# One fused transformer block: the end of a top-k routing step rearranged around the last batches of a shared network

## The chip, the cores and the metric

The kernel runs on one core of a Trainium2 chip. The metric is the device time of one execution in microseconds (us). The five engines of the core run their own instruction streams and wait for each other by semaphores: TensorE (PE, matmuls), VectorE (DVE), ScalarE (ACT), GpSimd (POOL) and SyncE (SP, which here only issues DMA transfers).

## The reference

The block takes 8 batches of 512 tokens with 256 features. Two conditioned layer norms stand ahead of a 16-head latent attention and of a mixture of experts; both results are added to the stream, scaled by gates. Only the second half matters here:

```python
scores = sigmoid(h @ gate_w.T)                 # 4096 tokens, 16 experts
topk_score, topk_ids = top_k(scores.T, 512)    # each expert takes its 512 best tokens
xin = h[topk_ids]
eo = silu(xin @ gw + gb) * (xin @ up_w + up_b) # F = 1024
eo = (eo @ down_w + down_b) * topk_score
out = zeros.at[topk_ids].add(eo)
shared = (silu(h @ sh_gate) * (h @ sh_up)) @ sh_down   # 512 wide, every token
x = x + gb_gate * (out + shared)
```

## The kernel before

The program has three parts in time: attention over 16 units of 8 heads (to about 440 us), the shared network over 8 batches (to about 610 us), and the 16 experts (to the end). Matmuls are made of three passes over values split into a high and a low part; ScalarE writes the high part, VectorE or POOL the low part. For a weight this split is called `cut`: ScalarE copies a quarter of a loaded piece, VectorE subtracts. An expert's gate, up and down weights are pieces of 1 MB that pass through two raw buffers, `WR`.

The shared network is a list of 48 steps, `ORDER`, and all five engines walk through it, `w` being the step's number. A step is either `glu(b, i)`, a quarter of the gate and up products of batch b (12 matmuls of 512 columns), or `down(b, i)`, half of its down product (24 matmuls of 256 columns). For b of 1 and more the order is glu 0, glu 1, glu 2, down(b-1, 0), glu 3, down(b-1, 1). So batch 6 begins at step 34 and batch 7 at step 40, and steps 46 and 47 are the down steps of batch 7. After a glu step, VectorE multiplies the two products into `HF` (L1688), ScalarE makes its high part `HTh`, POOL its low part `HTl` (L1925). After each quarter of a down step, VectorE makes the output rows: `tb` from the product and the gate row `GBt` (L1698), then `EO` as the sum with the batch's x2, `XL` (L1703). When a batch is done, SP stores `EO` and loads the next batch's `GBt` and `XL` into the same buffers (`store_out`, `load_xl`). `load_h` loads the split hidden state of a later batch into `XT`. Between steps 18 and 32 SP also copies gate rows into the table of token rows (`load_gate_rows`), 512 KB each.

From step 10 on the top-k runs between these products. Each engine counts ticks, four in a step; every third tick is a step `t` of the top-k. TensorE's ticks stand behind every third matmul of a glu step's quarter and behind each half of a down quarter. First the threshold of each expert is found bit by bit: VectorE counts the scores above a candidate (L1578), TensorE sums over partitions (L810), VectorE sets or drops the bit (L1567, L1570). At T_SEL VectorE marks scores above and equal to the threshold, at T_TIE it admits as many equal ones as are needed and runs a second prefix sum (`tensor_tensor_scan`, L1603), for which TensorE makes the offsets over partitions (L817). At T_POS the positions are formed and transposed by TensorE (L821). At T_VAL, T_HOT and T_VAL1, T_VAL2 VectorE makes, first for expert 0 and then for the others, the row and column of each position (`rows`), one-hot rows `OH` (`onehot`, four parts for an expert, L1661) and the token numbers as values `V4` (`values`). `index(x)` is 32 small matmuls of `OH` and `V4` (L877), from which VectorE writes `IDX` (L1671); POOL then gathers the 512 token rows of the expert into `XG` with four indirect DMAs (L1932). `turn(x, ck)` transposes them on TensorE (L892) and splits them into `XT`.

Each engine executes in order. The end of the list on VectorE reads:

```python
if w == W_INDEX:
    index(0)
...
if W_PIECES <= w < W_PIECES + 8:     # steps 39 to 46: gate and up weights of expert 0
    cut(e, piece_g(0) + j // 4, j % 4)
if w in (42, 43, 44, 45):
    onehot(1, w - 42)
```

The memory of expert 0's up weights holds the tables of the top-k until these are used up; the memory of its gate weights is free once the last batch's attention output is stored.

## Time and profile before

| | |
|---|---|
| median of 3 runs | 1196.64 us (1192.25 to 1196.66) |
| the profiled execution | 1189.41 us, its span 1187.7 us |
| busy share of the span | PE 94%, DVE 73%, POOL 53%, ACT 50% |
| mean granted TensorE clock | 0.966 of full speed |

The span goes from the first to the last instruction. Rows of a timeline show start and duration in us, engine, source line, operation, what is written and read, shape and count; brackets at the end give the time for which the engine stood idle before the row, and what it waited for. PE's durations overlap each other by a part of each matmul.

### The profile page before, as it was taken

Reading aid. Unit: us, or ns where it says so; the run is one execution under the profiler, and the core shown is the slowest. Engines: PE = TensorE matmul, PEld = TensorE weight load, DVE = VectorE, ACT = ScalarE, POOL = GpSimd, SP = SyncE. Lnnn points to the kernel's source line nnn. Section 1 sums busy time; section 2 is a strip of 40 time slices with the busy share of each in tenths; the row PEclk is TensorE's granted clock in tenths of the full one; section 3 lists DMA queues with packets and bytes.
Section 4 is the critical chain, followed back from the end, with each engine's and each line's share of the span. In section 5 each row is a group of like instructions: output and inputs, shape, how many; then the busy total and the mean of one; then the engine's idle time right before and its main releaser. Section 6 shows DMA issues by size and latency. Waiting matters only on the chain.

```text
span 1187.7 us, 21663 instructions
## 1 busy us (share of the span) xinstructions
PE 1115.0 (94%) x7463; PEld 868.7 (73%) x7464; DVE 865.0 (73%) x2213; ACT 596.9 (50%) x1083; POOL 634.0 (53%) x669
## 2 busy tenths in 40 slices
PE   7789989998988998998989999999999999999997
PEld 5455645555555567887778888888888888888886
DVE  5587888796877868887967767667767667767562
ACT  2257767776676654222334454344454444454441
POOL 4134476574665734222426656666656656656644
PEclk8788999998999999999989999999999999999999
DMA  7646677868668644857345555554455655455531
GB/s 192 89 72 118 109 122 161 175 126 173 132 149 167 175 149 130 256 183 212 95 141 122 139 155 132 145 135 127 135 154 133 143 136 126 136 154 134 139 81 18
DMA packets 100333, 165.44 MB, mean 139 GB/s; under 512 B 18424, under 2 KB 65016, under 8 KB 98176
## 3 DMA queue, kind: packets, MB, share of 16 engines
q1 hardware_dynamic: 83360, 137.04, 45.5%
q0 software_dynamic: 14336, 25.70, 11.2%
q10 hardware_dynamic: 2528, 1.32, 0.9%
q8 instruction: 60, 0.98, 0.4%
q14 instruction: 49, 0.40, 0.1%
HBM read 103.71 MB, written 34.11 MB: 116 GB/s over the span
## 4 chain that ended last, share of the span: by engine, by line
PE 58%; DVE 12%; DMA 10%; POOL 6%; issue 6%; SPq 3%; ACT 3%; ACTq 1%; DVEq 0%; POOLq 0%
PE MB L551 15%; PE LB L551 14%; PE LB L865 8%; PE MB L865 8%; DMA HT<-Us 3%; DVE junk L1319 3%; SPq L332 2%; PE XB L551 2%; PE LB L643 2%; PE UB L681 2%; PE UB L551 2%; POOL out_y L1967 2%; DMA rdD<-D 2%; DMA XT<-hD 1%; DMA DN<-rdD 1%
## 5 line engine op out<-in xcount | busy, mean ns | idle before, releaser
L1925 POOL TENSOR_TENSOR HTl<-HF,HTh 128x512 fp32r<-128x512 f32 x156 | 217.5, 1400 | 211.0 <-ACT HTh L1078 210.6
L1319 DVE CUSTOM_DVE_ANT_0 junk<-MB,MK 128x256 bf16<-128x256 f32 (+3 forms) x512 | 219.7, 483 | 62.7 <-PE MB L620 61.5
L1831 POOL TENSOR_SCALAR_AFFINE_SELECT P<-P 128x256 f32<-128x256 f32 x256 | 101.8, 422 | 153.8 <-ACT P L1017 153.6
L1967 POOL DMA_INDIRECT out_y<-EO,IDX x64 | 108.8, 1699 | 76.1 <-DVE EO L1787 66.0
L1089 ACT ACTIVATE SIL<-LB,gbT 128x512 f32<-128x512 f32 x64 | 43.9, 685 | 193.7 <-PE LB L551 193.7
L1015 ACT ACTIVATE P<-LB 128x768 f32<-128x768 f32 x128 | 103.7, 811 | 72.7 <-PE LB L643 72.5
L620 PE MATMUL MB<-KS,QS 48*128 48x256 f32 (+3 forms) x512 | 129.4, 365 | 9.9 <-DMA KS<-ST 4.7
L643 PE MATMUL LB<-QS,KS 50*128 50x256 f32 (+3 forms) x512 | 123.2, 358 | 15.4 <-ACT P L1015 12.5
L1078 ACT ACTIVATE HTh<-HF 128x512 fp32r<-128x512 f32 x156 | 97.8, 627 | 66.7 <-DVE HF L1688 66.4
L643 PEld LDWEIGHTS LB<-QS,KS 50*128 50x128 f32 x512 | 79.3, 192 | 63.4 <-issue 51.2
L620 PEld LDWEIGHTS MB<-KS,QS 48*128 48x128 f32 x512 | 81.4, 196 | 22.1 <-DVE NM L1319 12.4
L865 PE MATMUL LB<-WDh,HTh 128*128 128x256 f32 x320 | 94.0, 294 | 3.8 <-DVE tb L1698 3.8
L1688 DVE SCALAR_TENSOR_TENSOR HF<-MB,ubT,SIL 128x512 f32<-128x512 f32 x64 | 47.7, 745 | 66.0 <-ACT SIL L1089 30.4
L1661 DVE TENSOR_TENSOR OH<-R,iotab 128x1024 bf16<-128x1024 bf16 x64 | 93.1, 1458 | 0.0
L865 PE MATMUL MB<-WDh,HTh 128*128 128x256 f32 x320 | 92.0, 288 | 0.5 <-DVE tb L1698 0.5
L681 PE MATMUL UB<-P,V 128*32 128x512 f32 (+3 forms) x1024 | 90.9, 476 | 0.9 <-POOL P L1831 0.6
L865 PE MATMUL MB<-WDl,HTh 128*128 128x256 f32 x320 | 91.2, 285 | 0.0
L865 PE MATMUL MB<-WDh,HTl 128*128 128x256 f32 x320 | 91.1, 285 | 0.0
L865 PE MATMUL LB<-WDh,HTl 128*128 128x256 f32 x320 | 91.0, 284 | 0.0
L865 PE MATMUL LB<-WDl,HTh 128*128 128x256 f32 x320 | 91.0, 284 | 0.0
L1932 POOL DMA_INDIRECT XG<-tab,IDX x64 | 64.9, 1013 | 39.9 <-DVE IDX L1671 25.4
L1688 DVE SCALAR_TENSOR_TENSOR HF<-LB,ubT,SIL 128x512 f32<-128x512 f32 x64 | 47.7, 745 | 50.1 <-PE LB L551 50.1
(312 smaller groups left out, 3040.8 us busy)
## 6 DMA issues: line engine op xcount, KB each, us to landing
WR<-in_gw SPq DMA_DIRECT2D x16, 1024.0 KB, 7.6
WR<-in_uw SPq DMA_DIRECT2D x16, 1024.0 KB, 4.9
WR<-in_dw SPq DMA_DIRECT2D x16, 1024.0 KB, 5.5
QS<-ST SPq DMA_DIRECT2D x96, 128.0 KB, 4.6
KS<-ST SPq DMA_DIRECT2D x90, 128.0 KB, 5.9
hD<-h SPq DMA_DIRECT2D x8, 1024.0 KB, 5.8
XT<-hD SPq DMA_DIRECT2D x7, 1024.0 KB, 9.0
X<-in_x SPq DMA_DIRECT2D x8, 512.0 KB, 6.3
```

Source lines behind the costliest of these rows:

```text
L551: m = e.matmul(ps, a(c), r(c), start=(i == 0), stop=(i == 5))
L620: m = e.matmul(MB[:, o:o + w], QS[base:base + 48, k, i * 128:(i + 1) * 128], KS[base:base + 48, k, 0:w], start=True, stop=True)
L643: m = e.matmul(LB[:, o:o + w], KS[base:base + 50, k, j * 128:(j + 1) * 128], QS[base:base + 50, k, 128 * j:512], start=True, stop=True)
L681: m = e.matmul(UB[32 * h:32 * h + 32, 128 * j:512], V[b % 2][:, j, 8 * c + 4 * g + h, :], P[(8 * u + 4 * g + h) % NP][:, o:o + w], start=( ...
L865: m = e.matmul(ps, a[:, slots[f], ts], r[:, f, :], start=(f == 0 and t_ == 0), stop=(f == len(slots) - 1 and t_ == 2), skip_group_check=True)
L1015: e.activation(P[n % NP][:, 512:1280], LB[:, 512:1280], ACT.Exp).then_inc(a_p, 1)
L1078: e.activation(HTh[:, slot, :], hf_of(n)[:], ACT.Copy).then_inc(a_ht, 1)
L1319: m = e.tensor_tensor_reduce(junk[:, o:o + w], MB[:, o:o + w], MK[:, 512 - w:512], 1.0, -3e38, ALU.add, ALU.max, NM[:, k // 4, 4 * (k % 4) ...
L1688: e.scalar_tensor_tensor(out=hf_of(n)[:], in0=up, scalar=bias, in1=sil_of(n)[:], op0=ALU.add, op1=ALU.mult).then_inc(d_hf, 1)
L1831: m = e.affine_select(out=dd, in_=dd, compare_op=ALU.is_ge, fill=0.0, base=0, pattern=[[0, 2], [1, 128]], channel_multiplier=-1)
L1925: e.tensor_tensor(HTl[:, slot, :], hf_of(n)[:], HTh[:, slot, :].bitcast(F32), ALU.subtract).then_inc(g_ht, 1)
L1967: e.indirect_dma_start(out=out2, out_offset=bass.IndirectOffsetOnAxis(ap=IDX[x_ % 3][:, q:q + 1], axis=0), in_=EO[:, q, :], in_offset=None ...
```

## The change

The tie step's second matmul and all steps after it move by one top-k step: T_TIE keeps its work on VectorE, but TensorE takes its result one step (three ticks) later, and T_POS, T_VAL and the others follow one step later than before. The values of experts 1 to 15 are made in two halves in two steps. The first index moves from step 40 to 41 on all engines, and POOL's two halves of the first gather with it. The four cuts of expert 0's gate weights move to steps 18, 20, 22 and 24, those of its up weights are at steps 42 to 45. The down weights of expert 0 are loaded at step 34 instead of 43. Two of the four one-hot parts of expert 1 move into the first two quarters of expert 0; the second index moves there from quarter 1 to 2, and the one-hots of expert 2 by one quarter. The hidden state of batches 4 to 7 is loaded one step earlier. The last batch's x2 and gate row have buffers of their own, `XL7` and `GB7`, and are loaded at step 16.

```diff
 T_SEL = T_BIT + 31
-T_TIE, T_POS, T_VAL, T_HOT, T_VAL1, T_VAL2, T_END = (T_SEL + i for i in (1, 2, 3, 4, 6, 8, 9))
+T_TIE, T_POS, T_VAL, T_HOT, T_VAL1, T_VAL2, T_END = (T_SEL + i for i in (1, 3, 4, 5, 7, 8, 10))
+N_TIE, N_POS, N_VAL, N_ALL = (T_SEL + i for i in (2, 3, 4, 7))
...
 W_LOAD = 13
-W_PIECES = 39
-W_INDEX = 40
+W_CUTS = (18, 20, 22, 24, 42, 43, 44, 45)
+W_INDEX = 41
...
     SC6 = at("SC6", 50048, [128, 512])
+    XL7 = at("XL7", 33664, [128, 4, D])
+    GB7 = at("GB7", 37760, [128, D])
     VR = at("VR", 69504, [128, 8])
...
     c_gbt, c_xl, c_out, c_sco, c_pos, c_scat = (sem(n) for n in ("c_gbt", "c_xl", "c_out", "c_sco", "c_pos", "c_scat"))
-    c_sd = sem("c_sd")
+    c_sd, c_l7 = sem("c_sd"), sem("c_l7")
...
             e.dma_start(outv[b], EO[:]).then_inc(c_out, 16)
-            if b + 1 < NB:
+            if b + 2 < NB:
                 load_xl(b + 1)
...
                 store_split(NB - 1)
-            if kind == "glu" and i == 1 and 3 <= b < NB - 1:
+            if kind == "glu" and i == 0 and 3 <= b < NB - 1:
                 load_h(b + 1)
+            if w == 16:
+                e.wait_ge(c_xd, 16 * NB)
+                e.wait_ge(g_sd, 2)
+                e.dma_start(GB7[:], modD[NB - 1, 5:6, :].broadcast_to([128, D])).then_inc(c_l7, 16)
+                e.dma_start(XL7[:], xD[NB - 1]).then_inc(c_l7, 16)
             if w == 15:
...
                 e.dma_start(WR[1][:].rearrange("p (k n) -> p k n", k=2), kn(uw[0])).then_inc(c_wr[1], 16)
-            if w == W_PIECES + 4:
+            if w == 34:
                 load_piece(piece_d(0), dw[0])
...
                 e.matmul(XB[:, 2:3], Lm, PT[:, 511:512], start=True, stop=True).then_inc(p_top, 1)
-            elif t == T_TIE:
-                e.wait_ge(d_top, t + 1)
+            elif t == T_TIE + 1:
+                e.wait_ge(d_top, N_TIE)
                 e.matmul(XB[:, 3:4], Lm, PT[:, 511:512], start=True, stop=True).then_inc(p_top, 1)
             elif t == T_POS:
-                e.wait_ge(d_top, t + 1)
+                e.wait_ge(d_top, N_POS)
                 for k in range(4):
...
-            e.wait_ge(d_top, T_VAL + 3 if x_ else T_VAL + 1)
+            e.wait_ge(d_top, N_ALL if x_ else N_VAL)
             for k in range(32):
...
                 glu(n_eglu(x_, m_) - 1, m_, WG[x_ % 2], WU[x_ % 2], XT[x_ % 2], no_tick)
-                if nxt and m_ == 1:
+                if nxt and m_ == (1 if x_ else 2):
                     index(x_ + 1)
...
                 flush()
-            if W_PIECES <= w < W_PIECES + 8:
-                j = w - W_PIECES
+            if w in W_CUTS:
+                j = W_CUTS.index(w)
                 cut(piece_g(0) + j // 4, j % 4)
...
                 if t == T_HOT:
-                    e.wait_ge(d_top, T_VAL + 1)
+                    e.wait_ge(d_top, N_VAL)
                 onehot(0, 2 * (t - T_HOT))
                 rows(slice(1, NE), d_top)
-            elif t == T_VAL2:
-                values(slice(1, NE))
+            elif t in (T_VAL2, T_VAL2 + 1):
+                values(slice(1, NE), range(2 * (t - T_VAL2), 2 * (t - T_VAL2) + 2))
...
-        def values(es):
-            for q in range(4):
+        def values(es, qs=range(4)):
+            for q in qs:
                 e.tensor_scalar(of(V4[:, q, 0, :], es), of(GT[:], es), float(q), VR[:, 0:1], ALU.is_equal, ALU.mult)
...
             e.wait_ge(p_down, n)
-            e.wait_ge(c_gbt, 16 * (b + 1))
-            e.tensor_tensor(tb[q % 2][:], (LB, MB)[q % 2][:, 1024:1280], GBt[:], ALU.mult).then_inc(d_tb, 1)
+            last = b == NB - 1
+            if last:
+                e.wait_ge(c_l7, 32)
+            else:
+                e.wait_ge(c_gbt, 16 * (b + 1))
+            e.tensor_tensor(tb[q % 2][:], (LB, MB)[q % 2][:, 1024:1280], (GB7 if last else GBt)[:], ALU.mult).then_inc(d_tb, 1)
             e.wait_ge(d_tb, n)
-            e.wait_ge(c_xl, 16 * (b + 1))
+            if not last:
+                e.wait_ge(c_xl, 16 * (b + 1))
             if b:
                 e.wait_ge(c_out, 16 * b)
-            e.tensor_tensor(EO[:, q, :], tb[q % 2][:], XL[:, q, :], ALU.add).then_inc(d_eo, 1)
+            e.tensor_tensor(EO[:, q, :], tb[q % 2][:], (XL7 if last else XL)[:, q, :], ALU.add).then_inc(d_eo, 1)
...
                     shared_down(b, q)
-            if W_PIECES <= w < W_PIECES + 8:
-                j = w - W_PIECES
+            if w in W_CUTS:
+                j = W_CUTS.index(w)
+                if j == 4:
+                    e.wait_ge(d_top, N_ALL)
                 cut(e, piece_g(0) + j // 4, j % 4)
-            if w in (42, 43, 44, 45):
-                onehot(1, w - 42)
+            if w in (43, 45):
+                onehot(1, (w - 43) // 2)
         for x_ in range(NE):
                 glu(n_eglu(x_, m_) - 1, m_, ubT[:, x_, m_:m_ + 1])
+                if x_ == 0 and m_ < 2:
+                    onehot(1, 2 + m_)
                 if m_ < 4:
                     cut(e, piece_d(x_), m_)
-                if nxt and m_ == 1:
+                if nxt and m_ == (1 if x_ else 2):
                     index(x_ + 1)
                     cut(e, piece_g(x_ + 1), m_ - 4)
-                if x_ + 2 < NE and 2 <= m_ < 5:
-                    onehot(x_ + 2, m_ - 2)
+                if x_ + 2 < NE and (2 if x_ else 3) <= m_ < (5 if x_ else 6):
+                    onehot(x_ + 2, m_ - (2 if x_ else 3))
                 if nxt and m_ >= 6:
...
                     glu(n_eglu(x_, m_ - 1) - 1, m_ - 1, m_ - 1, n_edown(x_, 0) - 1)
-                if m_ == 1 and x_ + 1 < NE:
+                if m_ == (1 if x_ else 2) and x_ + 1 < NE:
                     index(x_ + 1)
             if x_:
```

## Rows read from the trace of the kernel before

**Rows 1.** Windows: busy us by engine, with instructions; then clock, DMA share, GB/s.

```profile
500.00:551.00 51.00, 50.88 (x313) 44.96 (x312) 40.88 (x121) 12.41 (x22) 14.19 (x11) 1.00 0.67 199
...
561.00:565.00 4.00, 4.00 (x12) 3.11 (x13) 1.51 (x3) 1.08 (x2) 0.00 (x0) 0.57 0.07 29
...
599.70:605.00 5.30, 5.23 (x24) 5.23 (x25) 4.16 (x7) 0.13 (x1) 0.81 (x1) 0.50 0.39 111
```

**Rows 2.** Timeline of PE, 552 to 612 us, the rows that begin with idle time.

```profile
552.37 0.72 PE L551 MATMUL LB<-XT,WG1h 128*128 128x512 f32 x2 [1.49 <-DMA XT<-hD]
...
560.96 0.38 PE L817 MATMUL XB<-PT,C 128*128 128x1 f32 x2 [2.36 <-DVE PT L1603]
...
575.84 0.99 PE L877 MATMUL UB<-V,OH 128*128 128x8 bf16 x32 [1.03 <-DVE OH L1661]
...
585.70 0.73 PE L551 MATMUL LB<-XT,WU1h 128*128 128x512 f32 x2 [1.91 <-DVE HF L1688]
...
594.90 0.39 PE L865 MATMUL MB<-WDh,HTh 128*128 128x256 f32 x1 [0.51 <-DVE tb L1698]
...
599.77 0.58 PE L865 MATMUL LB<-WDh,HTh 128*128 128x256 f32 x1 [2.60 <-DVE tb L1698]
...
607.21 0.39 PE L865 MATMUL LB<-WDh,HTh 128*128 128x256 f32 x1 [1.16 <-DVE tb L1698]
```

**Rows 3.** Timeline of DVE at the ties.

```profile
556.45 0.16 DVE L1594 TENSOR_SCALAR sm<-XB 128x1 f32<-128x1 f32 x1 [0.34 <-PE XB L814]
...
558.74 2.17 DVE L1603 TENSOR_TENSOR_SCAN PT<-GT,SC 128x512 f32<-128x512 f32 x1
```

**Rows 4.** DMA issues, KB and us to landing: issues of 534 to 541, then 497 to 501.

```profile
XT<-hD SPq DMA_DIRECT2D x1, 1024.0 KB, 15.8
```

```profile
XT<-hD SPq DMA_DIRECT2D x1, 1024.0 KB, 8.2
```

**Rows 5.** Chain of work that ended last, 470 to 700 us: start, us, what.

```profile
592.97 1.44 PE LB L865 x12
...
613.47 2.80 PE MB L551 x12
```

**Rows 6.** Timeline of DVE, 565 to 595 us.

```profile
565.57 0.69 DVE L1611 TENSOR_SCALAR PT<-UB 128x512 f32<-128x512 f32 x1 [2.64 <-PE UB L821]
...
568.92 2.36 DVE L1661 TENSOR_TENSOR OH<-R,iotab 128x1024 bf16<-128x1024 bf16 x2
...
575.71 0.40 DVE L1636 TENSOR_SCALAR GT<-PT 128x480 f32<-128x480 f32 x1
...
578.70 0.41 DVE L1698 TENSOR_TENSOR tb<-LB,GBt 128x256 f32<-128x256 f32 x1
...
580.29 0.68 DVE L1797 TENSOR_TENSOR WG0l<-WR,WG0h 128x512 fp32r<-128x512 f32 x1
...
581.08 0.16 DVE L1671 SCALAR_TENSOR_TENSOR IDX<-sm 128x4 uint32<-128x4 f32 x1
...
584.39 0.65 DVE L1646 SCALAR_TENSOR_TENSOR V<-GT,VB 128x480 bf16<-128x480 f32 x1
...
591.21 3.31 DVE L1703 TENSOR_TENSOR EO<-tb,XL 128x256 f32<-128x256 f32 x1
```

**Rows 7.** Timeline of POOL, 582 to 592 us.

```profile
582.19 1.46 POOL L1932 DMA_INDIRECT XG<-tab,IDX  x1 [8.96 <-DVE IDX L1671]
...
584.95 3.00 POOL L1925 TENSOR_TENSOR HTl<-HF,HTh 128x512 fp32r<-128x512 f32 x2
...
589.66 2.00 POOL L1932 DMA_INDIRECT XG<-tab,IDX  x1 [0.30 <-issue]
```

**Rows 8.** Tile XG, 575 to 640 us: us from issue to landing of its transfers.

```profile
DMA to landing us min/median/max: 3.6/3.8/6.8
```

**Rows 9.** Timelines of DVE and of PE at one bit step.

```profile
514.03 0.75 DVE L1578 TENSOR_SCALAR_CACHE_REDUCE jk<-S,si 128x512 bf16<-128x512 f32 x1
```

```profile
514.94 0.28 PE L810 MATMUL XB<-sm,C 128*128 128x1 f32 x2
```

## The prediction

> **What bounds the kernel now.** The windows come first. From 500 to 551 us TensorE has no gap to speak of: 50.88 of 51.00 us busy at clock 1.00 [rows 1]. So the bit steps of the top-k, shown as matmuls of one column between those of the shared network, cost it next to nothing, and what is added there costs only if a bit step comes late. Then TensorE's own timeline, read for the idle time in brackets: from 551 to 610 there are seven waits of over 0.5 us, one for a DMA and six for VectorE, 1.49 + 2.36 + 1.03 + 1.91 + 0.51 + 2.60 + 1.16 = 11.1 us [rows 2]. Back to the windows: two of the waits, 2.36 and 2.60, are followed by a stretch near or at the lower clock level, 4.00 us at 0.57 and 5.30 us at 0.50 [rows 1], where work that takes the full clock 2.3 and 2.65 us takes 4.00 and 5.30: 1.7 + 2.65 = 4.35 us lost. After waits of 1.49, 1.03 and 1.91 us no such stretch follows. So 15.4 us stand open between 551 and 610 us. Everything the diff touches either lies there or is moved out of there. VectorE's timeline [rows 3, 6] shows why it waits: VectorE does the ties, the rows, the one-hots and the values of the top-k one after another between the products that TensorE needs.
>
> **The hidden state of batch 6 (load_h one step earlier).** The transfer that TensorE waits for at 552.37 took 15.8 us to land; it stood behind a 512 KB copy of gate rows. The one for batch 4, issued just after the same output store and x2 load but ahead of all gate rows, took 8.2 [rows 4]. Moved to step i == 0 it is issued ahead of the gate rows of its own step. With a landing between 8 and 13 us (estimated from these two rows, with one copy less ahead) it is there by 549 and the wait goes. Bounds: 0 and 1.49 us gained. I take 1.4, less what the bit steps below lose, because a TensorE that arrives later waits less.
>
> **The ties in two steps.** TensorE's 2.36 us wait is for the second scan. VectorE's tie work runs from 556.45 to 560.91 (558.74 + 2.17) [rows 3]: 4.5 us, started by a TensorE matmul three products into step 35. Before, TensorE had nine products to do until it needed the scan; with the change it has eighteen. Twelve take 2.80 us [rows 5], so nine take 2.1: the second nine cover 2.1 of the 2.36, and about 0.4 is left with the small matmuls between. A wait of 0.4 is shorter than any that the clock fell after. Gain 1.9 plus the 1.7 of the slow stretch: 3.6 (bounds 1.9, if the clock falls all the same, and 4.1).
>
> **Everything behind the ties, three ticks later.** The position transposes move from step 36 to the middle of step 37; all of the top-k after them follows. I count from the end of these transposes. VectorE then does: value step of the first expert 2.75 (565.57 to 568.92, less a product of 0.60), a pair of shared outputs 1.6 (578.70 to 580.29), four one-hot quarters 4.6 (two in 2.36), a product 0.6, half a pair 0.8, the rows of the other experts 2.4 (575.71 to 578.70, less a product), half a pair 0.8, half the values 1.9 (eight from 581.24 to 585.04, halved), a product 0.6 [rows 6]. Together 16.1 us to the product of step 40, and 0.35 more to the index at the start of step 41. On top come collisions with POOL's split: a sum of two SBUF tiles beginning at 591.21 took 3.31 us where such a sum takes 0.4, while POOL ran without a break [rows 6, 7]. I add 1.0 (0 to 2.5).
>
> The Trainium skill says under "SBUF — State Buffer", section "Who interferes with whom", that a VectorE instruction with two SBUF inputs and a GpSimd one that reads SBUF exclude each other for a whole instruction. By that rule one-hots and weight splits, which have two SBUF inputs, could each lose up to a POOL split of 1.3 to 1.5 us, and the sum would tend to its upper end; the 3.31 us row agrees.
>
> TensorE meanwhile does 1.4 (half of step 37), 2.8, 2.9, 2.8 (steps 38 to 40), the first index 0.9, 2.8 (41), and half of step 42, 1.4: 15.0 us (12 gate/up products 2.80, 12 down products 1.44 [rows 5]; the index's 32 matmuls are the 0.99 us row at 575.84 [rows 2], 0.9 as the next ones overlap its end). There it needs the product of step 40, at 17.1: a wait of about 2 where 1.91 stood before (0.5 to 3.5). The wait of 1.03 for the one-hots goes: they are done 10.7 after the transposes, the index matmuls start at about 9.9 to 10; I keep 0.5 for it.
>
> **The first expert's gather.** VectorE's index stands at about 17.5. POOL then needs 0.95 to begin, two gathers 2.75 (582.19 to 584.95), two splits of the shared network 3.0, then 1.7 (587.95 to 589.66) to the issue of the last, and its landing: 3.8 us in the middle, 6.8 at worst [rows 7, 8]. The last gather lands 12 to 15 after the index, 29.5 to 32.5 after the transposes. TensorE comes to the turn of the gathered rows at 15.0 + 2.5 of waits + 1.4 + 2.9 + 2.8 + 2.9 = 27.5. So a wait of 2 to 5 us appears at step 46, which before had none. I take 2.5: the 1 MB down-weight load that ran beside the last gathers is now at step 34, and 3.8 is the nearer price. After a wait of that length the clock fell both times before; I take half of the second stretch's loss, 1.3 (0 to 2.65).
>
> **Gate weights among the bits.** A split is one ScalarE copy and one VectorE subtraction of 0.68 [rows 6]; four leave the crowded steps and go to steps 18, 20, 22 and 24. On VectorE the split of step 20 falls ahead of the count at 514.03, which ends at 514.78, and TensorE uses it at 514.94 [rows 9]: 0.16 of slack against 0.6 of work, so 0.5 us lost. At the other three the slack is larger. I take 0.5 (0 to 2.7, four whole splits). Removing them from the end is already in the sum above: steps 39 to 42 hold no gate splits.
>
> **x2 of the last batch in its own place.** Its two loads leave the end of step 45 for step 16, two more issues on SP, behind load_h and ahead of gate rows that are due only at the gather. The 1.16 us wait at 607.21 hangs on the late loads and goes; behind it only the output store of batch 6 is late, and I keep 0.3. The waits of 0.51 and 2.60 us are for VectorE's order and its 3.31 us sum; what is left of them is in the gather's wait above.
>
> **First expert.** Half the one-hots and the index of the second expert move there, one step later. VectorE was not the bound there; the gather is issued some 2 us later and is still down before its turn, four quarters of 2.8 us further on. I cost this at nothing; without that cover it is up to 2 us.
>
> **Sum.** Open before 15.4; left after: ties 0.4, one-hots 0.5, the product of step 40 2.0, gather 2.5, clock 1.3, end 0.3, bits and load_h 0.6, in all 7.6. So about 8 us come off. The span of 1187.7 becomes 1179.7; the profiled execution's 1189.41 becomes 1181.4. The median of the runs is 7.2 us above the profiled execution, so the forecast for it is 1196.6 − 8 = 1188.6, its own range 1185 to 1192.
>
> **Rivals.** *The gather decides all* (0.20): the index late by more collisions or a landing of 6.8, the clock down the whole 2.65. Wait 5 in place of 2.5, clock 2.65 in place of 1.3, other terms as above: gain 4, 1192.6, no difference to be told. For it: POOL's row of work without a break [rows 7]. Against: no weight load beside it now. *More than summed* (0.13): the gather in time and no fall of the clock: gain 8 + 2.5 + 1.3, about 12, 1184.6 or less. For it: TensorE's pure work behind the ties is fixed. *Slower* (0.05): the clock. Four waits of 0.4 to 2.5 us in 30 us of work; if it stayed at the lower level from step 42 to the first expert, about 17 us of full-clock work would take 17 more, 1205.6 in all. From 8 us of such work on nothing is gained, from 14 on the kernel is slower. Against: both stretches of before ended after 4 to 5.3 us, the last waits notwithstanding [rows 1]. *Change without effect*: not a case by itself; the 1.49 and 2.36 us waits have their cause in the order that is edited.
>
> The forecast has 0.62. What a measurement can tell is about 0.5%, 6 us, and the forecast stands only 2 us inside that. Faster by more: 0.62 + 0.13 less 0.04 at the forecast's edge, 0.71; within 0.5%: 0.24; slower 0.05. The range, 1180 to 1194, runs from below the better case to beyond the first rival.
>
> **To be seen in the profile after.** No wait for the hidden state before step 34; under 1 us at the tie matmul and no slow stretch behind it; a wait of 1 to 3 us at step 42's up half for the product of step 40; one of 2 to 5 us at the first turn, for the gathered rows; no wait for the last batch's x2. Wrong would make it: several bit steps late at 500 to 551 us, the gather landing later than 33 us after the position transposes, or experts longer than before.

## The result and the profile after

The changed kernel takes 1183.80 us (median of 12 runs, 1181.54 to 1194.76) against 1192.67 (12 runs, 1188.40 to 1201.29) for the kernel before beside it: ratio 0.9929, 95% interval 0.9901 to 0.9957. The medians are 8.9 us apart; the interval does not reach 1. The profiled executions, by which the prediction counted, went from 1189.41 to 1181.54 us, their spans from 1187.7 to 1179.8: 7.9 us less, where 8 were foreseen.

For everything below one stretch is used, called the stage: from the first bit sum that TensorE waits for behind 490 us to the first gate matmul of expert 0. It took 118.83 us before (491.59 to 610.42) and 111.34 after (491.33 to 602.67), so 7.5 of the 7.9 us came off there. The experts are the same: from the stage's end to the end of the span 577.28 us before and 577.13 after, the first expert 35.81 and 35.70.

The timeline of TensorE in the changed kernel, 510 to 604 us, the rows that begin with idle time (they answer to [rows 2]):

```profile
515.19 0.38 PE L821 MATMUL XB<-sm,C 128*128 128x1 f32 x2 [0.34 <-DVE jk L1590]
...
559.89 0.27 PE L829 MATMUL XB<-PT,C 128*128 128x1 f32 x1 [0.37 <-DVE PT L1615]
...
573.09 0.99 PE L889 MATMUL UB<-V,OH 128*128 128x8 bf16 x32 [0.36 <-DVE OH L1673]
...
581.15 0.74 PE L562 MATMUL LB<-XT,WU1h 128*128 128x512 f32 x2 [2.82 <-DVE HF L1700]
...
592.92 0.66 PE L904 MATMUL XB<-C,XG 128*128 128x128 f32 x4 [1.25 <-DMA XG<-tab,IDX]
...
594.86 0.39 PE L877 MATMUL LB<-WDh,HTh 128*128 128x256 f32 x1 [1.29 <-DVE tb L1714]
...
599.71 0.38 PE L877 MATMUL LB<-WDh,HTh 128*128 128x256 f32 x1 [1.00 <-DVE tb L1714]
```

These are seven waits, 7.43 us together, and no stretch at the lower clock; the prediction left 7.6 us of waits and lost clock. The one for the hidden state is gone, the tie's is 0.37 for 2.36, the one-hots' 0.36 for 1.03. The product of step 40 costs 2.82 instead of 1.91. The gather has a wait that it did not have before, and two waits for `tb` stand at the end, both behind late VectorE work.

The transfers of the hidden state, issued at 534 to 545 us, KB and us to landing (they answer to [rows 4]):

```profile
XT<-hD SPq DMA_DIRECT2D x1, 1024.0 KB, 9.9
```

VectorE's timeline of the changed kernel, rows at the bit step of step 20 and between 567 and 600 us (they answer to [rows 6] and [rows 9]):

```profile
512.61 0.68 DVE L1820 TENSOR_TENSOR WG0l<-WR,WG0h 128x512 fp32r<-128x512 f32 x1
...
514.38 0.75 DVE L1590 TENSOR_SCALAR_CACHE_REDUCE jk<-S,si 128x512 bf16<-128x512 f32 x1
...
567.32 5.72 DVE L1673 TENSOR_TENSOR OH<-R,iotab 128x1024 bf16<-128x1024 bf16 x4
...
574.78 2.33 DVE L1651 SCALAR_TENSOR_TENSOR GT<-PT,GT 128x480 f32<-128x480 f32 x2
...
581.20 0.16 DVE L1683 SCALAR_TENSOR_TENSOR IDX<-sm 128x4 uint32<-128x4 f32 x1
...
586.47 0.69 DVE L1700 SCALAR_TENSOR_TENSOR HF<-LB,SIL 128x512 f32<-128x512 f32 x1 [2.61 <-POOL HTl L1948]
...
589.69 2.45 DVE L1820 TENSOR_TENSOR WU0l<-WR,WU0h 128x512 fp32r<-128x512 f32 x1
...
594.84 1.34 DVE L1720 TENSOR_TENSOR EO<-tb,XL 128x256 f32<-128x256 f32 x1
...
599.89 0.43 DVE L1720 TENSOR_TENSOR EO<-tb,XL 128x256 f32<-128x256 f32 x1 [0.24 <-DMA out_y<-EO]
```

One row of the kernel before, with which the row of 2.33 us is compared:

```profile
576.14 1.35 DVE L1639 SCALAR_TENSOR_TENSOR GT<-PT,GT 128x480 f32<-128x480 f32 x2
```

POOL's timeline of the same kernel, 566 to 592 us (it answers to [rows 7]):

```profile
566.99 1.56 POOL L1948 TENSOR_TENSOR HTl<-HF,HTh 128x512 fp32r<-128x512 f32 x1 [4.54 <-ACT HTh L1090]
574.38 1.52 POOL L1948 TENSOR_TENSOR HTl<-HF,HTh 128x512 fp32r<-128x512 f32 x1 [5.83 <-ACT HTh L1090]
582.30 1.44 POOL L1955 DMA_INDIRECT XG<-tab,IDX  x1 [6.40 <-DVE IDX L1683]
584.05 0.97 POOL L1955 DMA_INDIRECT XG<-tab,IDX  x1 [0.31 <-issue]
585.04 2.56 POOL L1948 TENSOR_TENSOR HTl<-HF,HTh 128x512 fp32r<-128x512 f32 x2
...
589.31 0.95 POOL L1955 DMA_INDIRECT XG<-tab,IDX  x1 [0.30 <-issue]
590.28 1.30 POOL L1948 TENSOR_TENSOR HTl<-HF,HTh 128x512 fp32r<-128x512 f32 x1
```

Lay VectorE's and POOL's rows side by side. The four one-hots begin 0.33 us after a POOL split began and take 5.72 where [rows 6] give 4.6; the pair of rows at 574.78 begins 0.40 after the next split and takes 2.33 where the same two took 1.35 (576.14 in the kernel before); the 2.45 us weight split, 0.68 elsewhere, holds all of the POOL split of 590.28. And at 586.47 VectorE stands 2.61 us because POOL makes the low part of batch 7's first quarter only after the first two gathers.

### The profile page after: what moved, and what is told of

Same layout as the page of the kernel before. It is cut to its first block, busy times and chain, and to the rows that moved or that the text cites. A ratio compares the mean times of both kernels' runs of the same rounds, so it can differ in the third digit from the quotient of the medians.

```text
span 1179.8 us, 21665 instructions
## 1 busy us (share of the span) xinstructions
PE 1111.8 (94%) x7464; PEld 867.0 (73%) x7464; DVE 866.5 (73%) x2213; ACT 597.2 (51%) x1083; POOL 633.0 (54%) x669
## 4 chain that ended last, share of the span: by engine, by line
PE 62%; DVE 12%; DMA 6%; issue 6%; POOL 6%; ACT 4%; SPq 2%; ACTq 1%; DVEq 0%; POOLq 0%
PE MB L562 16%; PE LB L562 15%; PE LB L877 8%; PE MB L877 8%; DVE junk L1331 3%; PE UB L562 3%; PE LB L654 3%; PE XB L562 2%; DMA HT<-Us 2%; PE UB L692 2%; POOL out_y L1990 2%; SPq L337 1%; ACTq L1019 1%; POOL hl L1846 1%; DMA rdD<-D 1%
## 5 line engine op out<-in xcount | busy, mean ns | idle before, releaser
L692 PE MATMUL UB<-P,V 128*32 128x512 f32 (+3 forms) x1024 | 87.4, 461 | 0.7 <-POOL P L1854 0.4
```

Source lines behind the costliest of these rows:

```text
L692: m = e.matmul(UB[32 * h:32 * h + 32, 128 * j:512], V[b % 2][:, j, 8 * c + 4 * g + h, :], P[(8 * u + 4 * g + h) % NP][:, o:o + w], start=( ...
```

## The experiments

Each kernel is the changed one with an edit; each has one profiled execution, called its trace here. The whole time of a single execution varies by more than what is sought (1181.54 to 1194.76 us in the twelve of the change), so the traces are read by their stage. The change itself was run a second time (`after_again`): its stage is 110.47, so differences of under 0.9 us say nothing by themselves.

```
             stage  VectorE  clock, 4 us  what is altered
                    busy     behind the wait at step 42
before       118.83  98.65
after        111.34  97.24   1.00
after_again  110.47  96.62   0.57
u_load       111.43  96.77   0.62         hidden state one step later again
u_tie        114.64  97.40   1.00         ties in one step again
u_cuts       112.61  96.95   0.59         gate splits at steps 39 to 46 again
u_x2         115.17  96.91   0.60         x2 of the last batch as before
u_hot        112.31  98.45   0.61         four one-hots of expert 1 at 42 to 45
p_pool       111.15  98.94   1.00         first split ahead of the gathers
p_late       111.38  99.18   1.00         last value tables one step later
p_both       111.21  99.02   1.00         both, four gathers in a row
n_hot        107.97  93.23   0.58         no one-hot of expert 1 in the stage
n_hot2       108.54  93.36   0.58         the same, index of expert 1 later
n_hot2_late  108.04  94.89   1.00         n_hot2 with p_late
```

Clock is the granted clock of the windows view, a mean over the 4 us. At step 42 TensorE waits 2.82 to 2.85 us in nine of these traces; in six of them the clock then fell to 0.57 to 0.62 for 4 us, in three it stayed at 1.00. At 0.57 such a fall loses about 1.7 us where it stands, and later waits give part of it back (the wait for the gather was there in `after`, not in `after_again`). So each kernel is compared with the trace of the change that has the same clock there: 111.34 at 1.00, 110.47 at the lower one. This pairing was made after the traces were seen, and rests on one trace of the change at each clock.

The column shows step 42 alone. Four kernels have a further slow stretch before expert 0, which neither trace of the change has: `u_cuts` 0.62, `u_x2` 0.57 and `u_hot` 0.62, each for 4 us, and `p_both` 0.50 for 5.2 us. By these clocks it is worth some 1.5, 1.7, 1.5 and 2.6 us, an estimate, and it is part of what their stages show.

**u_load.** The hidden state is loaded at the step where it was before.

```diff
-            if kind == "glu" and i == 0 and 3 <= b < NB - 1:
+            if kind == "glu" and i == 1 and 3 <= b < NB - 1:
```

> The changed kernel with the hidden states of batches 4 to 7 loaded at i == 1 again; all else as changed. The stage is read from the matmul of the first bit sum that shows a wait (about 491 us) to the first matmul of expert 0: 118.8 us before, 111.3 changed. Theory (the transfer stood behind gate rows and set step 34): TensorE waits 1.3 to 1.6 us for the hidden state at step 34 again, and the stage is 1.0 to 1.5 us longer, 112.3 to 112.8. Rival (VectorE's count and mark work at the threshold is late anyway and hides it): no more than 0.4 longer.

Measured:

```profile
558.71 0.73 PE L562 MATMUL LB<-XT,WG1h 128*128 128x512 f32 x2 [0.98 <-DMA XT<-hD]
```

The wait is back with 0.98 us, and TensorE reaches step 42's product 0.95 later, counted from the stage's start (90.77 for 89.82), so nothing in between takes it up. It is less than the 1.49 of before because TensorE comes to it 0.6 later in the stage (59.89 for 59.29), while the transfer lands at the same place (60.87 and 60.78). The stage is 0.96 longer than that of `after_again`; against the 111.3 from which the expectation counts it is only 0.1 longer, as the rival has it.

**u_tie.** Both tie steps in one.

```diff
-            elif t == T_TIE + 1:
+            elif t == T_TIE:
```

> The changed kernel with TensorE's second tie matmul in the tie step itself, as before; the later top-k steps stay one step later. Theory: TensorE waits 2.4 to 2.7 us there in place of 0.37, everything behind is late by it: stage 2.0 to 2.3 us longer, 113.3 to 113.6; if the clock falls again after that wait, up to 1.7 more, 115.3. Rival (VectorE's row of work up to step 42 sets the end, so that TensorE's earlier wait is only moved): the 2.82 us wait at step 42 shrinks by what the tie wait grows, stage within 0.5 of 111.3.

Measured, two views of this kernel: TensorE's timeline, and the window behind its first row.

```profile
563.47 0.58 PE L829 MATMUL XB<-PT,C 128*128 128x1 f32 x2 [2.36 <-DVE PT L1615]
```

```profile
563.50:567.50 4.00, 4.00 (x12) 3.29 (x13) 1.40 (x3) 0.65 (x2) 0.00 (x0) 0.59 0.98 362
```

The wait of 2.36 is back to the hundredth, and so is the slow stretch of 4 us; at 0.59 it loses 1.6. The stage is 3.30 longer than the change's at the same clock later on. The prediction had 3.6, and this expectation up to 115.3 with the clock's fall.

**u_cuts.** The gate splits go back into steps 39 to 46, and the down-weight load with them.

```diff
-W_CUTS = (18, 20, 22, 24, 42, 43, 44, 45)
+W_CUTS = (39, 40, 41, 42, 43, 44, 45, 46)
...
-            if w == 34:
+            if w == 43:
```

> The changed kernel with the eight weight splits of expert 0 at steps 39 to 46 and its down weights loaded at step 43 again. Theory (VectorE is the bound from the transposes to the first index): two splits of 0.6 to 1.25 us stand ahead of the first index; the wait for the product of step 40 grows by 0.6 to 1.25, the index is 1.2 to 2.5 later, the last gather lands that much later, and the 0.34 us wait among the bits goes: stage 0.9 to 2.2 longer, 112.2 to 113.5. Rival (TensorE waits behind for POOL, not for VectorE's sum of work): stage 0.3 shorter.

Measured:

```profile
593.45 0.73 PE L562 MATMUL LB<-XT,WU1h 128*128 128x512 f32 x2 [3.43 <-DVE HF L1700]
...
608.21 1.11 PE L904 MATMUL XB<-C,XG 128*128 128x128 f32 x4 [3.10 <-DMA XG<-tab,IDX]
```

There is no wait at the bit steps of steps 18 to 24; the wait at step 42 is 3.43 and that for the gathered rows 3.10, with the clock at 0.59 and 0.62 behind them. The stage is 2.1 longer than `after_again`, a second slow stretch included. The splits and the down-weight load were put back together, so their shares are not told apart.

**u_x2.** The last batch's x2 is loaded into the buffers of the batch before, as it was.

```diff
-            if b + 2 < NB:
+            if b + 1 < NB:
                 load_xl(b + 1)
...
-            if w == 16:
+            if w == -1:
...
-            last = b == NB - 1
+            last = False
```

> The changed kernel with the last batch's x2 and gate row loaded into the shared buffers after the output store of batch 6, as before. Theory of the prediction: about 1.2 us, the wait of before at the second half of the last down step, less the 1.0 that stands there now: stage up to 1.2 longer, 111.3 to 112.5. Rival (now that the end is earlier, the load is on the path: store at 597.0, landing of the gate row 4.5 us after its issue at about 597.5, so the product with it at 602 in place of 599.2): 2.5 to 3.5 longer, 113.8 to 114.8.

Measured, VectorE's and then TensorE's timeline at step 46 of this kernel:

```profile
601.13 0.42 DVE L1714 TENSOR_TENSOR tb<-LB,GBt 128x256 f32<-128x256 f32 x1 [3.04 <-DMA GBt<-modD]
602.35 0.43 DVE L1720 TENSOR_TENSOR EO<-tb,XL 128x256 f32<-128x256 f32 x1 [0.80 <-DMA XL<-xD]
```

```profile
601.61 0.39 PE L877 MATMUL LB<-WDh,HTh 128*128 128x256 f32 x1 [4.14 <-DVE tb L1714]
```

SP issues the two loads at 596.27 and 596.76 and VectorE can go on at 601.13 and 602.35. The wait of 1.16 in [rows 2] was the visible end of this; with the other waits taken out ahead of it, TensorE comes there earlier, the wait is 4.14 and the clock falls to 0.57 for 4 us behind it. The stage is 4.7 us longer than that of `after_again` (3.8 longer than that of `after`), above the rival's 113.8 to 114.8 too, and far more than the 0.86 that the prediction read off the 1.16.

These four and `u_hot` (below), each undone alone, cost 0.96 + 3.30 + 2.1 + 4.7 + 1.8 = 12.9 us, against 7.5 to 8.4 that the whole change brings. The parts do not add up. The second slow stretches of `u_cuts`, `u_x2` and `u_hot`, about 4.7 us by the estimate above, are about as large as the surplus; whether one wait also hid part of the next in the kernel before is not shown. The later first index and the halved values were not undone alone.

**p_pool, p_late, p_both.** These try to remove what is left. In `p_pool` POOL makes the low part of batch 7's first quarter ahead of the first two gathers; in `p_late` the last value tables go from step 40 to the step after, behind the product of step 40; `p_both` does both and issues all four gathers in a row. Cuts from the edits:

```diff
 # p_late
-... for i in (1, 3, 4, 5, 7, 8, 10))
+... for i in (1, 3, 4, 5, 7, 9, 11))
 # p_pool: index(0, (0, 1)) moved behind the glu that precedes it on POOL
```

> The changed kernel with one order on POOL turned round: at step 41 the low part of batch 7's first quarter first, then the first two gathers of expert 0. Theory (VectorE's product of step 42 stands 2.61 us for that low part, which is queued behind the two gathers, and the waits of 1.29 and 1.00 us at the last down steps follow from it): VectorE's 2.61 us falls under 0.6, the two waits of TensorE together from 2.3 to under 0.6, the last gather lands about 0.8 later, and expert 0 begins 1.5 to 2.5 earlier: stage 109 to 110 where the clock stays up. Rival (the gather is what the end hangs on): expert 0 begins 0 to 0.8 later, stage 111.3 to 112.1. If the clock falls after the wait at step 42, as in three of the five looks so far, up to 1.6 more by either.

> The changed kernel with the values of experts 1 to 15 made one top-k step later, behind the product of step 40 and the first index on VectorE. Theory (VectorE's row of work from the transposes to that product is what TensorE waits for at step 42, and the index behind it sets the gather): the wait at step 42 goes from 2.82 to 0.8 to 1.0, the index is 1.9 us earlier, the last gather lands as much earlier, stage 1.5 to 2.0 shorter, 109.3 to 109.8. Rival (the low part on POOL behind the gathers sets the end, whatever is earlier on VectorE): stage within 0.5 of 111.3.

> Both at once, and all four gathers of expert 0 together behind the low part at step 41. Theory: the wait at step 42 under 1.0, POOL: low part to about 88.7 us from the stage's start, four gathers to 94, the last landing at 98 to 98.9; TensorE comes to the turn at 98.5 to 99, so no wait there over 0.5; no waits over 0.6 at the last down steps; stage 105.5 to 107, that is 4 to 6 us under the changed kernel, ratio to the kernel before 0.988 to 0.990. Rival (the gathers' issue or landing slows when four follow each other, or VectorE is late for the turn): stage 108 to 110, ratio 0.991 to 0.993.

Measured: the wait of VectorE (`p_pool`) or of TensorE at step 42 (`p_late`, `p_both`) that was aimed at went each time, and the stage, 111.15, 111.38 and 111.21, did not move. Rows of VectorE in `p_pool`:

```profile
585.48 1.50 DVE L1657 TENSOR_SCALAR V<-GT,VR 128x480 bf16<-128x480 f32 x1
...
589.47 1.77 DVE L1820 TENSOR_TENSOR WU0l<-WR,WU0h 128x512 fp32r<-128x512 f32 x1 [0.69 <-ACT WU0h L1075]
...
592.77 2.44 DVE L1820 TENSOR_TENSOR WU0l<-WR,WU0h 128x512 fp32r<-128x512 f32 x1
```

The 2.61 us idle row is gone, but 0.69 is now spent waiting for ScalarE's half of a split, a value row takes 1.50 for 0.46, and two weight splits take 4.21, where the change itself spent 3.52 on them (1.07 + 2.45) and two undisturbed ones take 1.36. TensorE's waits behind step 42 are 1.16 for the gathered rows and 1.35 and 0.99 for `tb`, as in the change. In `p_late` the wait at step 42 was 0.93 as expected, and waits of 0.53, 1.25, 1.12, 1.40 and 0.98 followed. In `p_both`, VectorE, then POOL, then TensorE and the window behind its row:

```profile
594.30 3.61 DVE L1820 TENSOR_TENSOR WU0l<-WR,WU0h 128x512 fp32r<-128x512 f32 x1 [0.69 <-ACT WU0h L1075]
```

```profile
592.62 0.96 POOL L1955 DMA_INDIRECT XG<-tab,IDX  x1 [0.30 <-issue]
593.88 0.95 POOL L1955 DMA_INDIRECT XG<-tab,IDX  x1 [0.30 <-issue]
594.86 2.50 POOL L1948 TENSOR_TENSOR HTl<-HF,HTh 128x512 fp32r<-128x512 f32 x2
```

```profile
598.30 0.58 PE L877 MATMUL LB<-WDh,HTh 128*128 128x256 f32 x1 [3.59 <-DVE tb L1714]
```

```profile
598.30:602.30 4.00, 4.00 (x18) 4.00 (x19) 3.97 (x7) 0.43 (x1) 0.00 (x0) 0.50 0.00 0
```

One split of 0.68 us stands through both POOL splits, TensorE waits 3.59 for `tb`, and the clock is 0.50 behind it. Without that slow stretch (2.6 us by the estimate above) the stage would be about 108.6, in the rival's 108 to 110, so this trace alone does not show that nothing was won. `p_both` was also timed: 1186.76 (6 runs), ratio to before 0.9910 (0.9875 to 0.9945), not to be told from the change's. The theory that one wait sets the end fell here. The next one was that VectorE's whole work between the ties and the last down step sets it: in these three its busy time in the stage is 98.9 to 99.2 us, 1.7 to 1.9 above `after`; what VectorE no longer stood idle went into stretched rows.

**after_again.**

> The changed kernel unaltered, beside the others on the same chip: ratio to the kernel before 0.990 to 0.996. Stage 111 to 112 by the theory that its waits are fixed by order; the wait at step 42 between 2.75 and 2.9 either way, and the clock after it either at 1.00 or near 0.6.

Measured: 1186.17 us (10 runs), ratio to before 0.9918 (0.9892 to 0.9944); stage 110.47, half a us under the expected band, with 0.57 behind the 2.82 us at step 42, no wait for the gathered rows, and two for `tb`:

```profile
599.30 0.39 PE L877 MATMUL LB<-WDh,HTh 128*128 128x256 f32 x1 [0.69 <-DVE tb L1714]
...
604.14 0.39 PE L877 MATMUL LB<-WDh,HTh 128*128 128x256 f32 x1 [0.99 <-DVE tb L1714]
```

**u_hot, n_hot.** Two one-hots of the second expert are put back into the stage, or the two that are left are taken out. `u_hot` also puts the second expert's index and the third one's one-hots back by a gate step; those lie behind the stage.

```diff
 # u_hot
-            if w in (43, 45):
-                onehot(1, (w - 43) // 2)
+            if w in (42, 43, 44, 45):
+                onehot(1, w - 42)
...
 # n_hot
-            if w in (43, 45):
-                onehot(1, (w - 43) // 2)
...
-                    onehot(1, 2 + m_)
+                    onehot(1, 2 * m_)
+                    onehot(1, 2 * m_ + 1)
```

> All four one-hot rows of the second expert stand at steps 42 to 45 again, as in the kernel before; nothing else is altered. Two more rows of 1.16 us each enter VectorE's work between the first expert's one-hots and the last down step (2.3 us, up to 3.5 with waits behind GpSimd), and the same two leave the first expert's gate steps. Theory (the sum of VectorE's work in this stretch, not one wait of it, sets when the first expert begins): the stage, 111.3 in the profiled run after and 110.5 in its repeat, becomes 112.8 to 114.8, with the loss in front of the two last down products (tb), not at step 42. Rival (the gathers and GpSimd's queue set the end, VectorE has room): the stage stays within 110.4 to 111.8. The whole time of one look varies by 3 us and decides nothing here.

> All four one-hot rows of the second expert stand in the first expert's first two gate steps (two in each); none is left at steps 43 and 45. Two rows of 1.16 us leave VectorE's work before the first expert. Theory (the sum of VectorE's work sets the start of the first expert): the stage becomes 108.0 to 109.5 from 110.5 to 111.4, and the first expert, in which TensorE had no wait, is longer by 0 to 1 us; ratio of the whole to the kernel before about 0.991 (0.9929 measured for the change). Rival (the last gather, 11.7 us behind the index, takes over as the limit): the waits of the two tb shrink and one for the gathered rows grows; the stage stays at 110 to 111.4. Second rival: the second expert's index comes late by the two rows, its gather lands after its first turn, and up to 2.5 us return as a wait at the second expert's first gate step.

Measured: `u_hot` is 1.8 longer than `after_again`, outside the rival's band and half a us short of the theory's, with the loss in front of `tb` as the theory has it:

```profile
599.42 0.58 PE L877 MATMUL LB<-WDh,HTh 128*128 128x256 f32 x1 [2.66 <-DVE tb L1714]
```

The waits for `tb` grew by 1.0 (2.66 for 0.69 + 0.99); the rest of the 1.8 goes with the slow stretch of 0.62 behind this wait. `n_hot` is 2.5 shorter, at the lower end that the theory names, and without a wait behind step 42. The windows of the stage in the change and in `n_hot` (us, then busy us of PE, PEld, DVE, ACT and POOL, then clock):

```profile
491.33:602.67 111.34, 103.78 (x654) 90.45 (x655) 97.24 (x230) 28.90 (x51) 33.42 (x26) 1.00 0.61 180
```

```profile
498.05:606.02 107.97, 104.04 (x655) 91.71 (x655) 93.23 (x228) 29.01 (x51) 33.17 (x26) 0.98 0.61 185
```

VectorE is busy 3.4 to 4.0 us less than in the change's two traces, 2.4 of it the two rows, the rest stretched rows. In the stage the two kernels differ from the change in these rows of VectorE alone, and it moves by them both ways: that VectorE's work behind step 42 holds up the end of the stage is shown by this pair. That the sum of its busy time sets the stage is not: `p_pool`, `p_late` and `p_both` have 98.9 to 99.2 us and stages of 111.2 to 111.4, `u_hot` 98.45 and 112.31, `u_x2` 96.91 and 115.17. And the whole did not gain: TensorE's timeline of `n_hot` in the first expert:

```profile
617.78 0.99 PE L889 MATMUL UB<-V,OH 128*128 128x8 bf16 x32 [3.23 <-DVE OH L1673]
```

The first expert took 40.62 us for 35.70, 3.23 of it this wait for the one-hots and the rest at a clock of 0.55 to 0.59 for some 4 us behind it. Neither the 0 to 1 us of the theory nor the second rival's place (the turn) was right. 1185.70 us, ratio 0.9910 (0.9877 to 0.9943).

**n_hot2, n_hot2_late.** The one-hots are spread over three gate steps and the index follows one step later.

```diff
-                if nxt and m_ == (1 if x_ else 2):
+                if nxt and m_ == (1 if x_ else 3):
                     index(x_ + 1)
...
-                if x_ == 0 and m_ < 2:
-                    onehot(1, 2 + m_)
+                if x_ == 0 and m_ == 0:
+                    onehot(1, 0)
+                if x_ == 0 and m_ < 3:
+                    onehot(1, 1 + m_)
```

> As n_hot, with the second expert's one-hot rows at the first expert's gate steps 0 (two), 1 and 2 and its index one gate step later (after step 3), on every engine that takes part. Theory: the stage stays at 107.5 to 109 as in n_hot (107.97), the 3.23 us that TensorE waited there for the one-hots before the index becomes 0 to 0.8, the gather lands some 22 us after the first expert's start, about when the second expert's first turn is due (23 us): 0 to 1 us of wait there. From the stage's first bit sum to the second expert's first gate step, which took 147.7 in the profiled run after and 146.6 in its repeat, 143.5 to 145.5; ratio of the whole to the kernel before 0.990 (about 2 us below the change's). Rival (VectorE is as full in the first expert as before it): the wait only moves on, to the index or to the second expert's turn, and the two stages together stay within 0.7 us of the change's.

> As n_hot2, and the last value tables stand one step later, as in p_late. In n_hot the one wait left in the end of the stage was the 2.83 us at step 42. Theory: p_late took 1.9 us of that wait away and lost them to VectorE's later work; with two one-hot rows less there is room for it, so the stage becomes 106.0 to 107.2. Rival (what p_late moves into VectorE's later work still comes back as waits for the last down products or for the gathered rows): the stage stays at 107.5 to 108.5, with 1 to 2 us of waits behind step 42.

(The two sums of 147.7 and 146.6 in the first expectation should have read 147.04, that is 111.34 + 35.70, and 146.23.)

Measured: stage 108.54 and 108.04, first expert 40.04 and 40.21 us. TensorE in `n_hot2`:

```profile
623.13 0.99 PE L889 MATMUL UB<-V,OH 128*128 128x8 bf16 x32 [1.73 <-DVE OH L1673]
...
634.82 0.66 PE L904 MATMUL XB<-C,XG 128*128 128x128 f32 x4 [2.24 <-DMA XG<-tab,IDX]
```

What the rival said happened: the wait only moved on, to the index (1.73) and to the turn (2.24). Stage and first expert together are 148.58 and 148.25 us (148.59 in `n_hot`, 148.03 in `u_hot`) against 147.04 and 146.23 for the change, so the loss is larger than the rival's 0.7. By these traces half the one-hots on each side is the best of the places tried, by 1.0 to 2.4 us; the timed ratios do not tell them apart. In `n_hot2_late` the wait at step 42 fell to 0.93 and 2.05 us came back behind it (0.31 + 1.29 + 0.45), as its rival said. The timed ratios, 0.9929 (0.9901 to 0.9958) and 0.9917 (0.9886 to 0.9949), cannot be told from the change's own. No kernel timed here beats it.

## Why the prediction was right, and where it was not

The forecast of 8 us less was met: 7.9 between the profiled executions, 8.9 between the medians. The median itself, 1183.80, is 4.8 under the 1188.6 forecast, 4.0 of it because the kernel before took 1192.67 beside it and not 1196.64. The waits for the ties, the one-hots, the product of step 40 and the gathered rows stand where the prediction put them; two at the end, for `tb`, it did not have. By its steps:

- **Hidden state.** The landing is 9.9 us, between the 8 and 13 given, and the wait is gone. Undone, it costs 0.96; the prediction took 1.4 less what the bit steps lose, 0.9 with its 0.5 for them.
- **Ties.** 0.37 left where 0.4 was forecast, clock 1.00 behind it; 3.30 when undone, for 3.6.
- **One-hots.** 0.36 for 0.5. They were done 10.1 us after the transposes (573.04 less 562.98). The prediction writes 10.7, which its own terms do not give: 2.75 + 1.6 + 4.6 is 8.95, and 9.95 with all of its 1.0 for collisions, so that no wait would be left by them. The one-hots alone were stretched by 1.1.
- **The product of step 40.** The mechanism was right, the term for collisions too small: from the end of the position transposes (562.98) to the end of this product (581.10) VectorE took 18.1, not 17.1 us. The two stretched groups above make 1.1 + 1.0 = 2.1 in place of the 1.0 that was taken, inside its bounds of 0 to 2.5. TensorE's wait is 2.82 for 2.0.

  The Trainium skill ("SBUF — State Buffer", section "Who interferes with whom") has a VectorE instruction with two SBUF inputs and a GpSimd one that reads SBUF exclude each other for a whole instruction. The trace agrees row by row: the 5.72, 2.33, 2.45 and 3.61 us rows each stand beside a POOL split. The 3.61 us row lost 2.9, more than the 1.3 to 1.5 of one split that the prediction worked out: both POOL splits in a row. By the same section of the Trainium skill the instruction that issues first gets the ports. The rows do not agree: the splits of 589.69 and 594.30 began before the POOL splits of 590.28 and 594.86, while POOL was issuing a gather (589.31 and 593.88), and were held all the same. What held them is open; POOL's times are rough in the profile.

- **Gather.** The index came at 18.4 for 17.5, the last landing at 29.9 after the transposes (592.9), inside 29.5 to 32.5; it took 11.6 us from the end of the index row, a little under the 12 to 15. TensorE itself came later, at 28.7 for 27.5. Hence 1.25 for 2.5, under the 2 to 5 that the prediction named as its sign, and nothing in `after_again`.
- **Clock.** 1.3 were kept for a fall behind the gather's wait. In the profiled execution none came; in `after_again` one came, but behind the wait at step 42. So the place was wrong, and that half a fall lies between the two is luck.
- **Gate weights among the bits.** 0.34 us at the step foreseen, for 0.5: the split at 512.61 stands ahead of the count at 514.38.
- **x2 in its own place, the end.** This is the step that failed: 0.3 left at the end became 2.29 (1.29 + 1.00). The output store, for which the 0.3 was kept, shows as 0.24 us on VectorE. But the prediction adds up VectorE's work only as far as the index and gives what stands behind it no term: it puts what is left of the old waits of 0.51 and 2.60 into the gather's wait. VectorE's row of work from step 42 on makes `tb` late: with two one-hots less in it (`n_hot`) both waits are gone. The 2.61 us that it stands for POOL's low part are not enough to explain them: in `p_pool` these are gone, and the waits are 1.35 and 0.99. The gain of the edit was mis-sized the other way, 3.8 to 4.7 for 0.86.
- **First expert.** Costed at nothing, and 35.70 for 35.81 us. `n_hot` shows that this held for two one-hots, not for four.

That the sum came out to 0.2 us (7.43 for 7.6) is luck: too much was kept for gather and clock (3.8 against 1.25) and too little for step 40 and the end (2.3 against 5.1), and the two errors cancel.

## What to carry to other kernels

Where VectorE runs a row of dependent work between products that TensorE needs, a wait that is reordered away can return at the next product, as in three kernels here; work moved out of the row shortened it. Busy time alone is no measure of that, since it contains what rows lose to another engine. A short wait in a trace is not the price of its cause: a late load that shows 1.16 us behind other waits was worth 3.8 to 4.7 us, a slow stretch included, once they were gone. Before work is moved into a stage that "has room", look at which engine has it there: two one-hots fitted into the first expert, four did not.

## What the runs showed of the hardware that was not expected

The same wait of 2.82 to 2.85 us at the same step was followed by a fall of TensorE's clock to 0.57 to 0.62 for 4 us in six traces of nine and by none in three. Rows of the windows view in `after` (no fall) and in `after_again`:

```profile
581.15:585.15 4.00, 4.00 (x27) 3.72 (x28) 2.67 (x7) 2.35 (x5) 2.52 (x3) 1.00 0.83 186
```

```profile
586.50:590.50 4.00, 4.00 (x15) 3.54 (x16) 2.69 (x6) 2.32 (x5) 2.56 (x3) 0.57 0.92 202
```

The length of the wait does not settle it either: behind a wait of 1.74 us that ended at 617.93 in `n_hot2_late` the clock was 0.50 for 2 us (620 to 622), behind 2.24 in `n_hot2` it stayed at 1.00. What decides between the two is open; no run here was made for it.
